# One root instead of a logarithm and an exponential, its square on GpSimd, and some copies handed to ScalarE, in a one-core transformer block

## The reference, cut to what matters

```
qkv = h @ w_qkv.T                                # h: normed x
attn = q k^T * 8**-0.5                           # 512 x 512 per head
x = attn - max(attn, -1)                         # so x <= 0
neg = 1 / (1 - x * (1 - 0.5 * x * (1 - x / 3)))  # the branch for x < 0
attn = neg / sum(neg, -1); out = attn @ v
x = x + ga * (out @ w_out.T + b_out)
h = norm(x) * (1 + cb) + sb
h = concat([h, -h]); h = relu(s0 * (h @ W0)) * 2; h = relu(s1 * (h @ W1)) * 2   # weights of +1 and -1
x = x + gb * s2 * (h @ W2)
```

## Time and profile before

| | us |
|---|---|
| median of 3 runs | 826.08 (824.42 to 827.48) |
| span of the profiled execution | 825.5 |
| busy: ACT, DVE | 705.7, 703.9 (85% each) |
| busy: PE, POOL | 647.8 (78%), 485.6 (59%) |

### The profile page before, as it was taken

The page is one execution under the profiler, slowest core; times in us unless marked ns, Lnnn a source line. Parts: engine busy times, 40 slices in busy tenths (PEclk is TensorE's granted clock), DMA queues, the critical chain, the costliest instruction groups (busy, mean ns, idle before and its releaser), DMA issues.

```text
span 825.5 us, 11417 instructions
## 1 busy us (share of the span) xinstructions
PE 647.8 (78%) x2847; PEld 226.8 (27%) x2897; DVE 703.9 (85%) x935; ACT 705.7 (85%) x620; POOL 485.6 (59%) x659
## 2 busy tenths in 40 slices
PE   3077777776787799779977898779977997895987
PEld 2022111211112234223422233223422342341344
DVE  5387998998989989999999999999999999975341
ACT  1007999999999999999999999999999999999610
POOL 7305766467666765777576775676567655673310
PEclk9999598889989999999999999999999999999999
DMA  3211111221031101310122102210131012000100
GB/s 80 72 60 46 59 37 35 63 72 37 16 91 58 52 2 42 102 66 22 43 80 72 35 15 77 82 53 1 56 85 62 16 43 72 6 5 6 48 23 13
DMA packets 34988, 39.28 MB, mean 48 GB/s; under 512 B 6376, under 2 KB 28160, under 8 KB 34944
## 3 DMA queue, kind: packets, MB, share of 16 engines
q1 hardware_dynamic: 34944, 38.77, 15.0%
HBM read 25.77 MB, written 8.40 MB: 41 GB/s over the span
## 4 chain that ended last, share of the span: by engine, by line
PE 29%; DVE 17%; ACT 16%; issue 15%; DVEq 1%; ACTq 0%
PE MB L453 10%; DVE mx L757 7%; DVE cub L745 6%; ACT prob L603 6%; PE OP L528 5%; ACT cub L590 5%; PE SA L504 4%; PE Z L483 4%; ACT sq L583 4%; PE SA L453 2%; DVE hid L778 1%; PE MB L462 1%; PE SA L462 1%; DVE OT L793 1%; PE MB L446 1%
## 5 line engine op out<-in xcount | busy, mean ns | idle before, releaser
L757 DVE TENSOR_REDUCE mx<-SA 128x2 f32<-128x1024 f32 (+1 forms) x277 | 302.4, 1097 | 38.9 <-PE SA L504 37.7
L745 DVE SCALAR_TENSOR_TENSOR cub<-sq,Z 128x1024 f32<-128x1024 f32 (+1 forms) x256 | 258.6, 1010 | 26.8 <-ACT sq L583 26.1
L583 ACT ACTIVATE sq<-Z 128x1024 f32<-128x1024 f32 (+1 forms) x256 | 232.1, 907 | 41.5 <-PE Z L483 41.1
L590 ACT ACTIVATE cub<-cub 128x2048 f32<-128x2048 f32 x128 | 251.0, 1961 | 2.6 <-DVE cub L745 1.7
L603 ACT ACTIVATE prob<-cub 128x2048 f32<-128x2048 f32 x128 | 250.4, 1956 | 0.2
L504 PE MATMUL SA<-KH,QH 96*128 96x512 bf16 x492 | 168.7, 406 | 93.2 <-DVE mx L757 45.2
L918 POOL TENSOR_TENSOR cub<-zc 128x512 f32<-128x512 f32 x96 | 99.9, 1040 | 172.2 <-DVE zc L740 156.0
L483 PE MATMUL Z<-QH,KH 128*128 128x512 bf16 x462 | 152.8, 405 | 50.2 <-DVE cub L745 42.0
L528 PE MATMUL OP<-prob,Vq 128*16 128x512 f32 x1024 | 145.0, 642 | 10.8 <-DVE OT L793 10.6
L923 POOL TENSOR_TENSOR cub<-cub,zc 128x512 f32<-128x512 f32 x96 | 122.7, 1278 | 8.0
L504 PEld LDWEIGHTS SA<-KH,QH 96*128 96x128 bf16 x492 | 44.2, 101 | 218.1 <-DVE mx L757 107.7
(11 more groups left out here) (130 smaller groups left out, 541.3 us busy)
## 6 DMA issues: line engine op xcount, KB each, us to landing
QH<-parts_q SPq DMA_DIRECT2D x96, 96.0 KB
KH<-parts_k SPq DMA_DIRECT2D x32, 288.0 KB
nd<-OT SPq DMA_DIRECT2D x128, 32.0 KB
parts_q<-SQ SPq DMA_DIRECT2D x24, 128.0 KB
parts_k<-SK SPq DMA_DIRECT2D x24, 128.0 KB
xa<-L_attn_x SPq DMA_DIRECT2D x8, 256.0 KB, 8.2
xb<-L_attn_x SPq DMA_DIRECT2D x8, 256.0 KB, 8.5
out<-y SPq DMA_DIRECT2D x8, 256.0 KB, 2.2
```

Source lines behind the costliest of these rows:

```text
L583: nc.scalar.activation(sq[:, h, part], Z[:, h, part], ACT.Square).then_inc(s_sq, 1)
L590: nc.scalar.activation(cub[:, m % F_RING], cub[:, m % F_RING], ACT.Ln, scale=-1.0, bias=2.0).then_inc(s_ln, 1)
L745: nc.vector.scalar_tensor_tensor(cub[:, n % F_RING, h, part], sq[:, h, part], 3.0, Z[:, h, part], ALU.add, ALU.mult).then_inc(s_cv, 1)
L757: nc.vector.tensor_reduce(mx[:, g % 2, j * TB + qts[0]:j * TB + qts[-1] + 1], logits_bank(b, beta, QUAD * g + j, qts[0])[:, qts[0] % 2:qts ...
```

## The change

1. 1/f as a reciprocal root: |f*f|^(-1/2). The logarithm of the whole head goes; in its place f is squared in place, by GpSimd for 13 heads of 16 (ON_POOL "P"), by ScalarE for heads 5, 10 and 15 ("A"), and ScalarE takes the reciprocal root of it.
2. So that f is a product without a constant beside it, the logit is shifted by the cubic's real root: the square gets a bias from a 128x1 tile (shift), the constant in cub is another, and the constant that ms adds is another.
3. No head has its first 512 columns made apart: zc, its copies and GpSimd's three instructions go. ScalarE squares and VectorE multiplies both whole halves.
4. cub has three places, and the square and the root follow their head by two steps (BEHIND = 2) instead of one.
5. The relus (L778) and the copy OT (L793) move from VectorE to ScalarE.
6. The layer norms' roots move from ScalarE to GpSimd, as a power of -0.5; 1/den becomes a square and a reciprocal root on ScalarE.
7. All batches are written out; the semaphore increments that set instructions apart in the loop go with it. A second activation table is loaded in set-up.

```
-PATHS = "VVDDVVAAVAVDVAAD"
+F_RING = 3
+ON_POOL = "PPPPPAPPPPAPPPPA"
+BEHIND = 2
+ROOT = -0.5960716379833215
+MAX_SHIFT = -(1.0 - ROOT)
+SQ_SHIFT = -1.5 * ROOT
+CUB_ADD = 3.0 + 0.75 * ROOT * ROOT
...
-                for b in range(FIRST, 3):
-                    body(b)
-                with eng.Fori(3, B - 2) as b:
-                    body(b)
-                for b in range(B - 2, B + 2):
+                for b in range(FIRST, B + 2):
...
             # ScalarE, from_z
-                if h == 0 and PATHS[n] == "A":
-                    nc.scalar.activation(zc[:, k % 2, :], Z[:, h, 0:S], ACT.Copy).then_inc(s_za, 1)
-                nc.scalar.activation(sq[:, h, part], Z[:, h, part], ACT.Square).then_inc(s_sq, 1)
+                nc.scalar.activation(sq[:, h, :], Z[:, h, :], ACT.Square, bias=shift[:, 0:1]).then_inc(s_sq, 1)
+            def square_of(n):
+                beta, m = behind(n)
+                if live(beta) and ON_POOL[m] == "A":
+                    need(act, s_cv, 2 * (H * beta + m + 1))
+                    nc.scalar.activation(f, f, ACT.Square).then_inc(s_fa, 1)
+            def prob_of(n):
+                    if ON_POOL[m] == "A":
+                        need(act, s_fa, N_A * beta + squares("A", m))
+                    else:
+                        need(act, s_fp, N_P * beta + squares("P", m))
+                    nc.scalar.activation(prob[:, m % P_RING, :], cub[...], RSQRT).then_inc(s_p, 1)
...
             for n in range(H):
                 from_z(n, 0)
-                log_of(n)
+                square_of(n)
+                relus(n, "sm")
                 misc(n, 0)
                 from_z(n, 1)
-                exp_of(n)
+                prob_of(n)
+                relus(n, "e")
+                take_numerators(n)
                 misc(n, 1)
...
             # GpSimd
+        def root_of(beta, mv, rs, s_ve, s_rs):
+            nc.gpsimd.tensor_tensor(rs[:, :], mv[:, :, 1], eps4[:, :], ALU.add).then_inc(s_ve, 1)
+            nc.gpsimd.wait_ge(s_ve, beta + 1)
+            nc.gpsimd.tensor_tensor(rs[:, :], rs[:, :], half4[:, :], ALU.pow).then_inc(s_rs, 1)
+            def square_of(n):
+                beta, m = (b, n - 1) if n else (b - 1, H - 1)
+                if live(beta) and ON_POOL[m] == "P":
+                    need(pool, s_cv, 2 * (H * beta + m + 1))
+                    nc.gpsimd.tensor_tensor(ff, ff, ff, ALU.mult).then_inc(s_fp, 1)
...
             for n in range(H):
-                from_z(n)
                 misc(n, 0)
+                square_of(n)
                 misc(n, 1)
```

More of the change, by code:

```diff
@@ L34, with squares @@
 FIRST = -1
-PATHS = "VVDDVVAAVAVDVAAD"
+F_RING = 3
 P_RING = 8
-F_RING = 2
+ON_POOL = "PPPPPAPPPPAPPPPA"
+BEHIND = 2
 LAG = 2
[L49 to L57, removed]
+ROOT = -0.5960716379833215
+MAX_SHIFT = -(1.0 - ROOT)
+SQ_SHIFT = -1.5 * ROOT
+CUB_ADD = 3.0 + 0.75 * ROOT * ROOT
+def squares(kind, n):
+    return ON_POOL[:n + 1].count(kind)
+N_P = squares("P", H - 1)
+N_A = squares("A", H - 1)
 CHUNKS = 4
@@ L602, in exp_of, with relus, relu_of, take_numerators @@
                     need(act, s_pv, QUAD * (NQ * beta + m // QUAD - 1))
-                    nc.scalar.activation(prob[:, m % P_RING, :], cub[:, m % F_RING].rearrange("p a n -> p (a n)"),
-                                         ACT.Exp, scale=-1.0).then_inc(s_p, 1)
+                    nc.scalar.activation(prob[:, m % P_RING, :], cub[:, (H * beta + m) % F_RING].rearrange("p a n -> p (a n)"),
+                                         RSQRT).then_inc(s_p, 1)
+            def relus(n, points):
+                if n == 0 and points[0] == "s" and isinstance(b, int) and b == B:
+                    for name, beta, bank in products_at(b - 1, H, "s"):
+                        if name[0] == "l":
+                            relu_of(name, beta, bank)
+                for name, beta, bank in products_at(b, n, points):
+                    if name[0] == "l":
+                        relu_of(name, beta, bank)
+            def relu_of(name, beta, bank):
+                layer, m = int(name[1]), int(name[3])
+                act.wait_ge(s_made[name], beta + 1)
+                last = "l1_3" if layer == 0 else "y"
+                if m == 0:
+                    need(act, s_made[last], beta)
+                nc.scalar.activation(hid[layer][:, m, :], bank, ACT.Relu, scale=sv[:, layer:layer + 1])\
+                    .then_inc(s_taken[name], 1)
+            def take_numerators(n):
+                if n % QUAD == (LAG + QUAD - 1) % QUAD:
+                    q = (n - LAG) // QUAD - 1
+                    beta, g = (b, q) if q >= 0 else (b - 1, q + NQ)
+                    if live(beta):
+                        i = NQ * beta + g
+                        act.wait_ge(s_pv, QUAD * (i + 1))
+                        need(act, s_gat[g % 2], (2 * beta + g // 2) * QUAD * 16)
+                        nc.scalar.activation(OT[:, g % 2, :], OP[:, :], ACT.Copy).then_inc(s_ot, 1)
             def misc(n, place):
@@ L735, in from_z @@
                     return
[L736 to L740 removed]
                 need(dve, s_sq, 2 * H * b + 2 * n + h + 1)
                 need(dve, s_p, H * b + n + 1 - F_RING)
[L744 to L745 removed]
+                nc.vector.scalar_tensor_tensor(cub[:, (H * b + n) % F_RING, h, :], sq[:, h, :], CUB_ADD, Z[:, h, :],
                                                ALU.add, ALU.mult).then_inc(s_cv, 1)
@@ L864, in dve_batch @@
                 from_z(n, 0)
-                if n == 0 and isinstance(b, int) and b == B:
-                    take_products(b - 1, H, "s")
                 take_products(b, n, "s")
```

152 lines of the change are left out of this document (44 added, 108 removed).

## The result

The changed kernel takes 835.87 us (835.01 to 837.43), the kernel before beside it 825.25 (822.24 to 827.48): ratio 1.0134, 95% interval 1.0105 to 1.0164. It is 1.3% slower; the forecast was 819 us, 0.9% faster. The profiled spans are 833.5 and 825.5 us, 8.0 apart and not 10.6. A run's time is 1.8 us above its span in the runs of the changed kernel (835.29 beside 833.5), so the profiled run of the kernel before, at 825.5, lies some 2 us above the median of its kernel.

What follows compares the result with a forecast made beforehand. ScalarE was taken as the bound in the middle, VectorE 2.7 us behind. From the 825.5 us span: +0.5 set-up, -8.6 batches 0 and 1, +6.5 batches 2 to 6, -6.5 batch 7, +1 tail: 818.4, forecast 819, range 796 to 841.

Steps and rivals of the forecast that it cites:

- knot: GpSimd's steps 1 to 5: splits and f*f squares queue, making ScalarE's root late; about 3 us a batch, batches 0 to 6.
- The prices: Full batch: f*f 3.6 us, reciprocal root 1.80; busy ScalarE 75.6, VectorE 79.5, GpSimd 73 us.
- Batches 0 and 1: First two batches: 81.6 and 83.2 us against 88.7 before, 8.6 us gained in all after weighting for half clock.
- That discount: Batches 0 and 1: nothing gained in TensorE's half-clock share, 0.38 and 0.24, so gains were weighted 0.62 and 0.76.
- small waits: ScalarE's steps with its own square of 2048 delay a cub by some 0.5 us a batch.
- TensorE's l1 steps: l1 steps stay 6.25 us long against 4.5 of VectorE's work, so VectorE waits 7.0 us a batch.
- The failed step: Batches 2 to 6: 79.5 + 7.0 + 3 + 0.5 = 90.0 us against 88.7, 6.5 us lost over five.
- The second failed step: Batch 7: 2 us gained in steps 0 to 7, 4.5 of ScalarE's 7 after; 6.5 gained, and tail +1.
- The first: Rival, GpSimd's steps 1 to 5: f*f costs 4.55 us, 3 us more a batch in seven batches; 840 us, chance 0.20.
- The second: Rival, full batches: knot and l1 excess mostly absorbed, a batch at 84.5 us; 790 us in all, chance 0.22.
- The third: Rival: hand-offs cost what engines save, or more half-clock stretches in batches 0 and 1; no change, 827 us, chance 0.13.
- The working note behind the sum: Full batch: VectorE's list becomes the new bound, 85.1 + 6.4 - 12.0 = 79.5 us.

Runs made afterwards that it cites:

- the dearer square: The changed kernel with f*f replaced by f times W1, a constant tile of the same shape: 862.73 us.
- The last version: Changed kernel with squares first on GpSimd, batch 7's x1n there, head 2 also squared on ScalarE, only l0 relus of batches 2 to 6 on ScalarE: 809.17 us.

## Why the prediction was wrong

- **What bounds the kernel before: right, but not the whole of it.** ScalarE's work filled 87.6 of 88.8 us, and taking 10.9 us a batch from it moved the waits to VectorE, which went from 3.7 us of waits for squares and logits to 11.6. But a second limit lay close behind: no version of this document with full l1 products brought a full batch under 88.4 us, with ScalarE at 72 to 78. So the change could win little in batches 2 to 6 even without a knot.
- **The prices: right.** f*f 3.60 (3.6), the root 1.91, ScalarE 76.7 (75.6), VectorE 80.3 (79.5), GpSimd 74.3 (73) a batch. The same-tile row was the one to read; the dearer square shows what the other would have meant.
- **Batches 0 and 1: right in kind,** 10.8 gained for 8.6. They take 80.9 and 83.2, where the forecast had 81.6 and 83.2 before it took something off for the half clock. That discount did not show; the clock rose (0.87 and 0.94 now, 0.81 and 0.88 in the earlier trace rows). On the other side the kernel before had stood at 87.2 and 87.7 there, not at the 88.7 that was set against them.
- **The knot in GpSimd's steps 1 to 5: the right place and order, too small a price.** The ends of the two squares were forecast 7.5 us apart and are 7.3. Forecast 3 us a batch and 0.5 for small waits, with head 2's root alone late; VectorE waits 4.7 for squares, 3.5 of it behind two late roots, those of heads 1 and 2. On top comes the 1.35 us at TensorE's half clock behind the knot, for which the forecast had no term. That the knot's idle time brought it is not shown: with x1n moved, one batch had the same idle time at full clock, and with the knot gone some batches still had a half-clock stretch. The order with f*f first, which keeps all work and all prices, takes 17 us off. In its trace 14.0 lie in batches 2 to 6, of which some 2.6 are two batches at full clock. The knot is shown as the largest cause there.
- **TensorE's l1 steps: right in kind.** Forecast 7.0, measured 6.9 for all of VectorE's waits for logits, of which 1.35 is the half clock's behind the knot. The l1 steps' own part is about 5.5, which is also what mx waits in every full-clock batch of the other versions with whole l1 products and the relus on ScalarE, and halving l1 gave 5.0.
- **The failed step is the sum for batches 2 to 6:** 90.0 forecast, 92.4 measured. Of the 2.4, VectorE's list is 0.8 and its waits for squares 1.2 (4.7 for 3.5); the 1.35 of the half clock is offset by the smaller l1 part; the last 0.4 to 0.5 is in two small waits of VectorE that had no term, ms for the transposed maxima (0.3) and mx with no releaser in the profile (0.2). Over five batches, and with the kernel before at 89.1 on average there and not 88.7, +6.5 became +16.4.
- **The second failed step is batch 7:** 6.5 forecast for it and +1 for the tail, 5.5 won; measured 0.8 won up to step 12 and 2.7 lost from there on, 1.9 lost. I had reckoned ScalarE's chain as the only bound, and of the 7 us that it gives up I had counted 4.5 as won. ScalarE did give up 5.7 us up to step 12 (65.55 to 59.84), and the stretch kept 0.8. One part is shown: an x1n held for the length of an f*f (3.3 us in the trace, 2.3 in the time). Another is the relus' place, 1.7 us in the tail at equal clock. The clock is the third: in the tail, where TensorE is nearly alone, half-clock stretches make about 1.7 us in each of its two pieces (43.3 against 41.6, 29.1 against 27.5). The last version has the one at the end too, with its relus there on VectorE, and two versions with the relus on ScalarE end without it. So the relus' engine doesn't decide the one at the end, and what does stays open.
- **From span to time:** I added 0.6 us, the distance to the median; in the runs it is 1.8. This makes 1.2 of the miss.
- **The rivals.** The first (f*f at 4.55, 840 us) had the time nearly right and the cause wrong: the cause it named needed the dearer square, which gave 863. The second, that the waits would be absorbed, fell in the kernel after. The third had something of the truth in the wrong place: half-clock stretches did cost, but in batches 2 to 6 and in the tail, while the clock of batches 0 and 1 rose. The working note behind the sum, that VectorE's list is the bound, is half wrong: putting the relus back moved 4.6 us of work onto it at no cost to a full batch, and splitting them took 2.2 off for 0.2. Work there and waits there changed places. So moving relus off VectorE, counted in the forecast at 5.4 us a batch, was worth nothing in a full batch, while it put them into ScalarE's order behind the roots.

What stays open: with the knot gone and the clock full, a full batch takes 88.4 to 88.6 us in four versions whose VectorE has between 80.2 and 84.7 us of work, whose GpSimd has 70.8 or 74.4, and whose TensorE has about 75; the kernel before stands at 88.8. Halving l1 showed that TensorE's l1 steps are part of what sets it; that they are all of it was not shown, because that cut was made only with the knot in place.

## What to carry to other kernels

Giving an engine longer instructions is judged by the order around its existing bursts, not by its busy share: GpSimd was at 74 of 92 us, and the place of one call in its loop was worth 17 us, more than the 10.6 that separate the two kernels. An engine's own list is a lower bound of the period and not a term of it, so before counting an instruction that leaves, see whether that engine waits soon after; if it does, the wait takes its place. And look for a second cost behind a wait that leaves TensorE idle: in all five full batches of the changed kernel a half-clock stretch came with it, at about 1.3 us each, though the same wait was also seen without one.

## What the runs showed of the hardware

GpSimd's product of a 128x2048 tile with itself takes 3.60 us, with another tile 4.54. A VectorE TENSOR_SCALAR from SBUF to SBUF was held until GpSimd's running instruction ended. The two clear places in the changed kernel are x1n in batch 7 (3.6 us for 0.34), and in set-up xn beside two memsets:

```profile
6.37 7.17 DVE L681 TENSOR_SCALAR xn<-xa,mv,rs 128x128 f32<-128x128 f32 x4
```

against 1.11 us for the same four with GpSimd idle (802.43), while VectorE's cub, with an operand in PSUM, ran through beside f*f at its usual 1.21 us. It isn't SBUF operands as such that are held: four BATCH_NORM_STATS2 of xa took 0.87 us beside a memset, 0.86 elsewhere, and four BATCH_NORM_AGGREGATE 0.37 beside an f*f. The Trainium skill (GPSIMD Engine Reference, section 1, Specifications) says that the two engines share their SBUF interface and contend for some VectorE instructions; the trace agrees, and shows VectorE alone paying in these two places, in both of which it met an instruction that GpSimd was already running. A relu of a PSUM bank takes 0.69 us on ScalarE and 0.74 on VectorE.
